# Two later input loads moved from ScalarE's DMA queue into the queue of the stores

## The reference

```
B, F, E = 2048, 32, 64
i_idx, j_idx = triu_indices(F, k=1)              # 496 pairs
xw = einsum('bfe,ed->bfd', x, W)
out = xw[:, i_idx, :] * x[:, j_idx, :]           # (2048, 496, 64) float32
```

## Time and profile before

| what | before |
|---|---|
| time, median of 3 runs | 650.51 us (649.46 to 650.63) |
| time of the profiled execution | 650.77 us |
| its span, first to last instruction | 649.0 us |
| bytes moved by DMA in the span | 277.01 MB, mean 427 GB/s |
| busy share: VectorE | 88% |
| busy share: TensorE, ScalarE | 25%, 22% |
| DMA packets of q1, share of 16 engines | 95.9% |
| DMA packets of q10, share of 16 engines | 3.1% |
| stores: number, median from issue to landing | 48, 26 us |
| later loads: number, median from issue to landing | 2, 26.8 us |

### The profile page before, as it was taken

One profiled execution on the slowest core, in us unless ns is written; L12 is line 12 of the kernel. 1 busy time (PEld: TensorE's weight loads), 2 busy tenths in 40 slices (PEclk: granted clock), 3 DMA queues, 4 the chain that ended last, 5 costly groups with the idle time before them and its releaser, 6 DMA issues.

```text
span 649.0 us, 2591 instructions
## 1 busy us (share of the span) xinstructions
PE 162.9 (25%) x776; PEld 82.2 (13%) x776; DVE 568.5 (88%) x528; ACT 140.2 (22%) x259; POOL 0.7 (0%) x6
## 2 busy tenths in 40 slices
PE   5614060605006042050600604114060411300000
PEld 3302030302003011020300302002030200100000
DVE  3999999999579999999857999899999989999940
ACT  4523050505005041130500505023050502301000
POOL 0000000000000000000000000000000000000000
PEclk9958575756657657585755756758575665855555
DMA  9999999999999999999999999999999999999996
GB/s 390 421 417 452 424 445 427 421 449 405 404 454 420 449 423 421 453 419 448 429 422 446 429 420 453 419 437 437 422 452 418 430 447 417 452 424 423 451 420 283
DMA packets 8092, 277.01 MB, mean 427 GB/s; under 512 B 1040, under 2 KB 1040, under 8 KB 1040
## 3 DMA queue, kind: packets, MB, share of 16 engines
q1 hardware_dynamic: 7632, 268.44, 95.9%
q10 hardware_dynamic: 448, 8.42, 3.1%
HBM read 16.81 MB, written 260.05 MB: 427 GB/s over the span
## 4 chain that ended last, share of the span: by engine, by line
DMA 51%; DVE 43%; issue 2%; PE 0%; DVEq 0%; ACTq 0%; ACT 0%
DMA out_dram<-out_ring 50%; DVE out_ring L268 43%; DMA W_sb<-in_W_dram 1%; PE xwT_ps L154 0%; DVEq L60 0%; ACTq L235 0%; ACT xw_first L206 0%; DVEq L264 0%
## 5 line engine op out<-in xcount | busy, mean ns | idle before, releaser
L268 DVE TENSOR_TENSOR out_ring<-xw_rest,x_sb 128x832 f32<-128x832 f32 (+21 forms) x384 | 323.1, 917 | 16.3 <-DMA out_dram<-out_ring 16.3
L268 DVE TENSOR_TENSOR out_ring<-xw_first,x_sb 128x1984 f32<-128x1984 f32 (+2 forms) x144 | 247.0, 1781 | 38.6 <-DMA out_dram<-out_ring 27.6
L173 PE MATMUL xwT_ps<-xT_sb,W_sb 64*64 64x512 f32 x252 | 85.1, 759 | 389.1 <-ACT xT_sb L212 389.1
L232 ACT COPY xw_rest<-xw_ps 128x512 f32<-128x512 f32 x48 | 28.1, 586 | 427.1 <-DVE out_ring L268 425.7
L218 ACT COPY xwT_sb<-xwT_ps 64x512 f32<-64x512 f32 x126 | 73.3, 582 | 11.7 <-PE xwT_ps L173 11.0
L173 PEld LDWEIGHTS xwT_ps<-xT_sb,W_sb 64*64 64x64 f32 x252 | 14.6, 159 | 402.6 <-ACT xT_sb L212 392.9
L183 PE MATMUL xw_ps<-identity,xwT_sb 128*128 128x128 f32 x252 | 48.5, 323 | 29.6 <-ACT xwT_sb L218 29.6
L146 PE MATMUL xT_ps<-identity,x_sb 128*128 128x128 f32 x256 | 45.6, 309 | 5.6 <-DMA x_sb<-in_x_dram 5.6
L183 PEld LDWEIGHTS xw_ps<-identity,xwT_sb 128*128 128x128 f32 x252 | 31.1, 160 | 94.7 <-ACT xwT_sb L218 79.2
L212 ACT COPY xT_sb<-xT_ps 128x512 f32<-128x512 f32 x63 | 37.2, 590 | 2.2 <-PE xT_ps L146 0.9
L146 PEld LDWEIGHTS xT_ps<-identity,x_sb 128*128 128x128 f32 x256 | 36.3, 163 | 6.9 <-issue 5.6
(11 more groups left out here) (1 smaller groups left out, 0.1 us busy)
## 6 DMA issues: line engine op xcount, KB each, us to landing
out_dram<-out_ring SPq DMA_DIRECT2D x32, 5280.0 KB, 26.1
out_dram<-out_ring SPq DMA_DIRECT2D x16, 5312.0 KB, 25.4
x_sb<-in_x_dram ACTq DMA_DIRECT2D x2, 4096.0 KB, 26.8
x_sb<-in_x_dram SPq DMA_DIRECT2D x4, 1024.0 KB, 7.8
x_sb<-in_x_dram SPq DMA_DIRECT2D x1, 4096.0 KB, 19.6
W_sb<-in_W_dram ACTq DMA_DIRECT2D x2, 16.0 KB, 5.9
```

The costliest lines, as they stand in the source:

```text
L173: nc.tensor.matmul(xwT_ps[s % 2][odd][rows, :, :], W_sb[rows, :], xT_sb[s % 2][rows, :, :], start=True, stop=True).then_inc(projected[odd], 1)
L232: nc.scalar.copy(xw_of(t, g), xw_ps[s % 2][:]).then_inc(xw_copied, 1)
L268: last = nc.vector.tensor_tensor(slot[:, place:place + n, :], one.to_broadcast([LANES, n, E]), x_sb[buf][:, r, j:j + n, :], ALU.mult)
```

## The change

The block that issued a later load in ACT's `copy_xw` is taken out. SP issues the same load, into the same buffer and with the same semaphore, right after it has issued the last store of the tile that frees the buffer. ACT's wait for `chunk_ready` stays. Bytes, number of DMAs and all other instructions stay.

```diff
                     sp.dma_start(out_tiles[g, r, :, q0 * E:q1 * E],
                                  out_ring[c][:, 0:(q1 - q0) * E]).then_inc(stored[c], 16)
+                if r == ROWS - 1 and g + XBUFS < LOADS:
+
+                    sp.dma_start(x_sb[g % XBUFS][:], x_loads[g + XBUFS]).then_inc(x_landed[g + XBUFS][0], 16)
...
                 if g == 1 and t > 0:
 
                     act.wait_ge(chunk_ready, t * CHUNKS)
-
-                    done, r = divmod(t - 1, ROWS)
-                    if r == ROWS - 1 and done + XBUFS < LOADS:
-                        act.dma_start(x_sb[done % XBUFS][:], x_loads[done + XBUFS]).then_inc(
-                            x_landed[done + XBUFS][0], 16)
                 act.wait_ge(turned_back, s + 1)
```

## The result

The changed kernel takes 651.05 us (median of 22 runs, 650.69 to 651.37). Beside it the kernel before took 650.14 (22 runs, 649.22 to 650.77). The ratio is 1.0013 with a 95% interval of 1.0008 to 1.0019: a small loss, under the 0.2% that was named as the bound of "no change", but clear of the scatter. The forecast was 650.3, a change of -0.2 from the 650.51 of the first three runs; its range held the time; its sign was wrong.

The account below looks back on a forecast made before the run. The prediction took the full DMA engines as the bound. From the profiled 650.77 us, three terms of 0 and -0.4 for mixing gave 650.4, stated as a median of 650.3; range 649.0 to 651.6.

Parts of the forecast that it names:

- What bounds the kernel: Whole span: the DMA engines have no gap left to fill; a tile without a load takes 37.76 us.
- ACT's and SP's issues: Two load issues leave ACT (0.36 us each) and join SP (0.33 to 0.48 each), under cover of waits: 0.
- later arrival: The load lands some 34 us after issue, not 25.9 to 27.7; its first reader has 59 us to spare: 0.
- rival C: Behind the load in the store queue, VectorE's next chunk isn't ready: up to 11.8 us per load, up to 674; chance 0.02.
- Seams: Passes between store and load in one queue: 0.1 to 0.2 us each, four make 0 to 0.8; taken as 0.
- Rival B: Store queue doesn't overlap passes between store and load: 2.3 us for each load, 655.4 in all; chance 0.09, whole or part.
- A load costs the same in either way: At the later loads: a 4 MB load takes 9.7 us of DMA time, alone or beside stores.
- the moved load: At tiles 3 and 7, the load stands between stores instead of beside them; the VectorE stall only changes chunk: 0.
- What the mixing costs now: At load 2 beside stores, 0.75 to 1.8 us looked lost; the new order was to give back 0.4 us.
- rival A: At load 2, reads and writes sharing the engines hinder each other; the new order stops it: 649.0 us; chance 0.19.
- From the sum to the median: Last step: the 650.4 for the profiled execution, 0.26 above the median of 650.51, was turned into a median of 650.3.

Follow-up runs that it names:

- Four pieces in the store queue: The changed kernel with each later load cut into four 1 MB pieces, one behind each of four successive stores: 651.29 us, ratio 1.0026 to the kernel before.
- the kernel with the small read: The changed kernel plus a 32 KB read of the input in the store queue behind tile 1's last store, some 75 us before load 2: 651.01 us.
- those on ACT's queue: The kernel before with each later load in four 1 MB pieces on ACT's queue, each issued once its rows are free: 649.51 us, ratio 0.9996.

## Why the prediction was wrong

**What bounds the kernel:** right. The DMA engines stay full in both kernels, and the chain has the same shares (51% DMA, 43% VectorE).

**ACT's and SP's issues, later arrival, no starving:** right. The first issue in the store queue took SP 1.25 us, more than the 0.48 that I took (and more than the 0.81 that stands in the same rows for L116), under the same cover. The loads landed after 34.1 and 34.7 us (33 to 35 forecast), VectorE waited 11.43 and 10.01 us (about 10 forecast; the first has the stall in it), and nothing showed of rival C.

**Seams, taken as 0:** right. Load 3's two seams cost 0.1 us (85.39 against 85.29 above), within the 0.2 for each that the prediction gave as its bound. Four pieces in the store queue, with 16 passes in place of 4, took 0.28 us more than the kernel with the small read, which ran in the same group. Rival B's 2.3 us for each load are nowhere. The Trainium skill's "DMA: Bandwidth & Descriptors" fits, in its section on the anatomy of one DMA, a fixed 2.0 us for a DMA that GpSimd issues. By these 0.28 us it is no price for each entry of this queue.

**"A load costs the same in either way":** this step failed. Its two witnesses were the load at the start and load 3, and neither of them has the stall. For the first later load (load 3 as the only one) the runs show 9.80 us beside the stores and 11.09 in their queue. In the sum this is the term of the moved load, taken as 0; it is about +0.9 with both loads and +1.3 with one. The prediction had the two stretches in view but took its price from the load that wasn't stretched: it let the third store of tile 3 land 9.7 us sooner without load 2 ahead of it, where it landed 10.93 us sooner (34.05 - 23.12).

**"What the mixing costs now", taken as -0.4:** wrong in sign and in what it is. I read the 10.45 us of load 2's packets and the 419 GB/s as a cost that the mixing might cause and that the new order might give back. The stall is there without mixing as well (414 GB/s), so rival A is gone. The forecast that GB/s would be flat at 433 to 435 through both loads failed at load 2 alone. And these rows are means over 16 engines, while the end goes by the last one. Of the 1.8 us that the mean showed as lost, the kernel before had paid only about 0.5 (19.9 against 19.4 us for two lone loads); in the store queue it is 1.5 (20.9). So the sum gave back time of which little was on the path, and the new order put more of it there.

**From the sum to the median:** the 650.4 was for an execution of 650.77; less the same 0.4, the median of 650.51 gives 650.1 and not 650.3. That the range held the measured time owes something to its width: the 0.8 at its upper end was meant for seams, which cost little.

**What stays open.** Why the first later load stalls, and a second one doesn't, is not settled. It is neither the data, nor the place in SBUF, nor the time since the start, and small reads at the start or 75 us ahead don't take it away. A larger read ahead of it wasn't tried by itself. Why the last engine escapes a part when the load has its own queue is not shown either, nor whether it is one and the same engine throughout. That it takes two queues, and not just a finer order, is suggested by the pieces: in the store queue 651.29, on ACT's queue 649.51; but those on ACT's queue were also issued earlier.

## What to carry to other kernels

Where all DMA engines are full, moving a transfer between queues can still cost time. Here the load in the queue of the stores passed its whole delay on to the store behind it, while beside them in a queue of its own a part of that delay didn't reach the engine that ends last. A mean over the engines (share, GB/s) shows that packets were slow, not that the end was later; for that, compare when the same store lands in two kernels, one of them without the transfer. And a price measured on one transfer of a kind should not be used for another whose own rows show something else.

## What the runs showed of the hardware that was not expected

The first 4 MB load after a long stretch of stores alone is slow in every profile that has one, wherever it reads and writes: its 50 us move 412 to 426 GB/s. The second such load, some 160 us later, is not: 430 to 435 where both loads are whole. And the 16 DMA engines drift apart over a kernel: in the changed kernel the first of them has done its share of the third store of tile 2 at 134.89 us and the last at 136.81; for the last store of all these are 642.77 and 648.80. Of these six microseconds the last three belong to one engine alone: the second to last is done at 645.77.
